# Attention on one core: three steps change engine, two places of waiting move, and two later stages load and square their rows in pieces

## The reference, cut to what matters

```python
x = x + attention_a(layernorm(x))      # changed: phase_attend
x = x + moe_ffn(layernorm(x))
x = x + attention_b(layernorm(x))      # changed: first loads (phase_route), squares and first loads (phase_final)
x = x + moe_ffn(layernorm(x))
```

```python
out_t = softmax(local_scores) @ v
pcs   = (softmax(causal_scores) * exp(index_decays)).sum(rows of a segment)
kv    = einsum(normalised_scan(pcs), k, v);  out_lin = q @ kv
y     = tw * out_t + (1 - tw) * out_lin
```

```python
o = o * rsqrt(mean(o * o, -1) + EPS) * norm_w      # 4 heads of 64 per token
o = o * silu(x @ w_g);  out = o @ w_o
```

## Time and profile before

| | |
|---|---|
| time of 3 runs, median (lowest to highest) | 2725.63 us (2721.02 to 2728.28) |
| the profiled execution: its own time, its span | 2726.8 us, 2725.1 us |
| busy over the span | PE 85%, DVE 72%, ACT 57%, POOL 45% |
| attention a | 137 us to 1289 us: 32 heads |
| phase_route | 1603 us to about 1722 us |
| phase_final | 2342 us to about 2436 us |

### The profile page before, as it was taken

One profiled execution on the slowest core, in us unless ns is written; L12 is line 12 of the kernel. 1 busy time (PEld: TensorE's weight loads), 2 busy tenths in 40 slices (PEclk: granted clock), 3 DMA queues, 4 the chain that ended last, 5 costly groups with the idle time before them and its releaser, 6 DMA issues. The chain is left out here.

```text
span 2725.1 us, 72677 instructions
## 1 busy us (share of the span) xinstructions
PE 2308.1 (85%) x27120; PEld 1534.0 (56%) x27120; DVE 1961.8 (72%) x4896; ACT 1543.3 (57%) x3579; POOL 1220.2 (45%) x2149
## 2 busy tenths in 40 slices
PE   8689999999999999997987944499999999678792
PEld 5444444444444444444765844377777777566681
DVE  6478888888888898886564656277777776477465
ACT  5467777777777777775352322266666665236230
POOL 3323333333333333334775536544444544247561
PEclk9879999999999999999998975599999999689896
DMA  6711111111112111110447645301111111443555
GB/s 218 241 39 38 38 38 37 32 35 34 38 38 65 38 38 38 32 37 9 152 157 200 228 156 178 119 21 47 47 49 49 50 39 32 166 159 132 155 157 198
DMA packets 187257, 243.43 MB, mean 89 GB/s; under 512 B 41256, under 2 KB 144565, under 8 KB 184992
## 3 DMA queue, kind: packets, MB, share of 16 engines
q1 hardware_dynamic: 160512, 182.07, 21.8%
q0 software_dynamic: 19872, 50.41, 5.4%
q10 hardware_dynamic: 6528, 6.31, 0.8%
HBM read 136.09 MB, written 106.50 MB: 89 GB/s over the span
## 5 line engine op out<-in xcount | busy, mean ns | idle before, releaser
L658 DVE TENSOR_REDUCE at_mn<-at_S 128x1 f32<-128x1024 f32 (+4 forms) x704 | 604.4, 878 | 118.3 <-PE at_S L767 118.0
L588 ACT ACTIVATE at_E<-at_S,at_mn 128x1024 f32<-128x1024 f32 (+4 forms) x704 | 591.4, 850 | 162.9 <-DVE at_mn L658 162.8
L807 PE MATMUL at_pcs<-at_E,at_c 128*32 128x256 f32 (+1 forms) x4864 | 432.9, 345 | 0.0
L767 PE MATMUL at_S<-at_sk,at_sq 96*128 96x512 bf16 (+3 forms) x1152 | 334.2, 354 | 48.6 <-ACT at_E L588 25.1
L540 POOL TENSOR_TENSOR at_kvo<-at_kh,at_vh 128x256 f32<-128x256 f32 x512 | 303.7, 627 | 0.1
L578 ACT ACTIVATE at_Tt<-at_S,at_mn 128x192 f32<-128x192 f32 x512 | 173.7, 422 | 134.1 <-DVE at_mn L648 134.1
L807 PEld LDWEIGHTS at_pcs<-at_E,at_c 128*32 128x32 f32 x4864 | 185.8, 108 | 86.5 <-issue 80.6
L520 POOL TENSOR_TENSOR at_fi<-at_f,at_inv 128x12 f32<-128x12 f32 x128 | 26.3, 206 | 443.0 <-DVE at_inv L675 443.0
L1287 POOL DMA_INDIRECT expert_out<-m_ysb,m_dst x158 | 155.4, 984 | 129.1 <-DVE m_dst L1465 115.8
L767 PEld LDWEIGHTS at_S<-at_sk,at_sq 96*128 96x128 bf16 x1152 | 78.5, 97 | 231.5 <-issue 92.3
L807 PE MATMUL at_pcs<-at_Tt,at_c 128*32 128x128 f32 x1024 | 208.7, 286 | 0.0
(11 more groups left out here) (392 smaller groups left out, 5552.6 us busy)
## 6 DMA issues: line engine op xcount, KB each, us to landing
m_xg<-expert_rows SPq DMA_DIRECT2D x158, 129.0 KB
at_sq<-q_parts SPq DMA_DIRECT2D x192, 64.0 KB, 2.3
at_sk<-k_parts SPq DMA_DIRECT2D x192, 64.0 KB, 2.2
memory_rows<-m_blank SPq DMA_DIRECT2D x8, 1032.0 KB, 4.5
gl_hx<-memory_rows SPq DMA_DIRECT2D x32, 258.0 KB, 3.5
m_wgu<-in_f_wgu SPq DMA_DIRECT2D x2, 4096.0 KB, 14.4
rt_yin<-expert_out SPq DMA_DIRECT2D x8, 1024.0 KB, 10.4
fn_yin<-expert_out SPq DMA_DIRECT2D x8, 1024.0 KB, 8.1
```

What stands on the lines that cost most here:

```text
L588: nc.scalar.activation(E[:, at:at + w], S[v % NS_B][:, 0:w], ACT.Exp, bias=mn[:, q, s, 1 + j:2 + j], scale=-1.0, accum_out=rs[:, q, s, 1 + ...
L658: nc.vector.tensor_reduce(mn[:, q, s, 1 + j:2 + j], S[v % NS_B][:, 0:w], AX.X, ALU.min).then_inc(s_mn, 1)
L767: ins = nc.tensor.matmul(S[v % NS_B][:, c:c + cw], sq[:, u, t * P:(t + 1) * P], sk[:, u, c0 + c:c0 + c + cw], start=True, stop=True)
L807: ins = nc.tensor.matmul(pcs[j * R:(j + 1) * R, cols[0]:cols[1]].rearrange("p (b c) -> p b c", c=P), lhsT, rhs, start=(n, j) not in touche ...
```

## The change

In `phase_attend`:

- The difference (minima minus top) goes from VectorE (`tops`) to GpSimd (`differences(g + 1)`, at the end of turn g).
- The copy of the turned tiles goes from VectorE (behind minima 2) to ScalarE (behind exponential 2).
- `factors(g)` goes from the end of turn g-1 to a place behind exponential 1 of turn g.
- `outputs(g)` goes from behind minima 3 to behind minima 4.

In `phase_final` the square becomes 16 activations of 64 columns, each with its sum, and the sum on VectorE goes. In `phase_final` and `phase_route` the first step's loads are issued tile by tile, and the first mix waits tile by tile. TensorE's order is the same before and after.

```diff
+            def differences(g):
+                pool.wait_ge(s_top, g + 1)
+                pool.tensor_tensor(diff[:, g % 2, :, :], mn[:, g % NQ, :, :],
+                                   top[:, g % 2, :].unsqueeze(2).to_broadcast([P, NQ, KK]), ALU.subtract
+                                   ).then_inc(s_diff, 1)
...
+            def keep_transposed(g):
+                act.wait_ge(s_TT, 2 * g + 2)
+                if g >= 2:
+                    act.wait_ge(s_O, g - 1)
+                nc.scalar.copy(TTs[:, g % 2, :], M[:, :]).then_inc(s_TTs, 1)
...
                     for k in range(1, 1 + last):
                         exps(g + 1, k)
+                        if k == 1:
+                            factors(g)
+                        if k == 2:
+                            keep_transposed(g)
...
-                    factors(g + 1)
...
                 for k in range(1, 1 + len(units[(g + 1) % NQ])):
                     minima(g + 1, k)
-                    if k == 2:
-                        keep_transposed(g)
                     if k == 3:
                         inverses(g)
+                    if k == 4:
                         outputs(g)
```

```diff
+                if n == 0:
+                    for t in range(G):
+                        sp.dma_start(o[:, 0, t, :], o_dram[t * P:(t + 1) * P, :]).then_inc(first_in[t], 16)
+                        sp.dma_start(yin[:, 0, t, :], yb[t * P:(t + 1) * P, :]).then_inc(first_in[t], 16)
+                    return
...
-                nc.scalar.activation(sq[:, n % 2, :], o[:, n % NB, :, :].rearrange("p t d -> p (t d)"), ACT.Square
-                                     ).then_inc(s_sq, 1)
+                for r in range(G * GH):
+                    ins = nc.scalar.activation(sq[:, n % 2, r * GV:(r + 1) * GV], o[:, n % NB, r // GH, r % GH * GV:(r % GH + 1) * GV],
+                                               ACT.Square, accum_out=ss[:, n % 2, r:r + 1])
+                ins.then_inc(s_sq, 1)
...
-                nc.vector.tensor_reduce(ss[:, n % 2, :], heads(sq[:, n % 2, :]), AX.X, ALU.add).then_inc(s_ss, 1)
```

More of the change, by code:

```diff
@@ L544, in products @@
                     ins.then_inc(s_kvo, 1)
+            differences(0)
             for g in range(NG):
@@ L554, in _ @@
                     products(n - 1, 10, NT)
+                if g + 1 < NG:
+                    differences(g + 1)
             products(NHEAD - 1, 5, NT)
@@ L615, in _ @@
                 exps(0, k)
-            factors(0)
             for g in range(NG):
@@ L629, in _ @@
                             keep_kvr(n - 1)
-                    factors(g + 1)
+            factors(NG - 1)
+            keep_transposed(NG - 1)
             keep_pcs(NHEAD - 1)
@@ L1674, in phase_route @@
         y_in = [m.sem(f"y_in{u}") for u in range(NB)]
+        first_in = [m.sem(f"first_in{t}") for t in range(G)]
         s_stat, s_var, s_rstd, s_hn = (m.sem(k) for k in ("stat", "var", "rstd", "hn"))
@@ L1805, in stats_of @@
                 u, t0 = n % NB, first_tile(n)
-                dve.wait_ge(y_in[u], (n // NB + 1) * 16)
+                if n:
+                    dve.wait_ge(y_in[u], (n // NB + (u > 0)) * 16)
                 for j in range(TOPK):
@@ L1810, in stats_of @@
                     for t in range(G):
+                        if n == 0 and j == 0:
+                            dve.wait_ge(first_in[t], 16)
                         nc.vector.scalar_tensor_tensor(acc[:, t0 + t, :], yin[:, u, t, j * D:(j + 1) * D],
@@ L2667, in phase_final @@
         o_in, y_in = ([m.sem(f"{k}{u}") for u in range(NB)] for k in ("o_in", "y_in"))
+        first_in = [m.sem(f"first_in{t}") for t in range(G)]
         h_in = [m.sem(f"h_in{u}") for u in range(2)]
-        s_g, s_silu, s_mix, s_sq, s_gated, s_ss, s_inv, s_y = (
-            m.sem(k) for k in ("g", "silu", "mix", "sq", "gated", "ss", "inv", "y"))
+        s_g, s_silu, s_mix, s_sq, s_gated, s_inv, s_y = (
+            m.sem(k) for k in ("g", "silu", "mix", "sq", "gated", "inv", "y"))
         s_T, s_yT, s_zmm, s_z = (m.sem(k) for k in ("T", "yT", "zmm", "z"))
@@ L2753, in mix @@
                 u = n % NB
-                dve.wait_ge(o_in[u], (n // NB + 1) * 16)
-                dve.wait_ge(y_in[u], (n // NB + 1) * 16)
+                if n:
+                    dve.wait_ge(o_in[u], (n // NB + (u > 0)) * 16)
+                    dve.wait_ge(y_in[u], (n // NB + (u > 0)) * 16)
                 for j in range(TOPK):
@@ L2759, in mix @@
                     for t in range(G):
+                        if n == 0 and j == 0:
+                            dve.wait_ge(first_in[t], 32)
                         nc.vector.scalar_tensor_tensor(o[:, u, t, :], yin[:, u, t, j * D:(j + 1) * D],
@@ L2770, in gate_rows @@
                                         silu[:, n % 2, :], ALU.mult).then_inc(s_gated, 1)
-            def sums(n):
-                dve.wait_ge(s_sq, n + 1)
-                if n >= 2:
-                    dve.wait_ge(s_inv, 2 * n - 3)
-                nc.vector.tensor_reduce(ss[:, n % 2, :], heads(sq[:, n % 2, :]), AX.X, ALU.add).then_inc(s_ss, 1)
             def norm(n):
@@ L2795, in _ @@
             gate_rows(0)
-            sums(0)
             mix(1)
@@ L2800, in _ @@
                     gate_rows(n + 1)
-                    sums(n + 1)
                 norm(n)
```

15 lines of the change are left out of this document (3 added, 12 removed).

## The result

| | before | after |
|---|---|---|
| median (lowest to highest) | 2726.95 us of 4 runs (2721.02 to 2728.78) | 2888.97 us of 4 runs (2887.68 to 2892.04) |
| span of the profiled execution | 2725.1 us | 2886.0 us |
| mean granted clock of TensorE | 0.922 | 0.904 |

The ratio is 1.06, with a 95% interval of 1.0583 to 1.0617: the change makes the kernel 162 us slower. The forecast was 2847 us and at most 2880.

What follows compares the result with a forecast made beforehand. Attention a was taken to run at a ring of window exponentials, scores and minima, not at VectorE. 127 us more there, 5 off in `phase_final` and 1 off in `phase_route` gave 2847 us, range 2780 to 2880.

Steps and rivals of the forecast that it cites:

- The ring: Attention a's loop: window exponentials (ScalarE), scores 3 to 5 (TensorE), minima 5 and 6 (VectorE); 35.29 us per four turns.
- The rival in which VectorE is the bound: Attention a: copy and difference come off each turn, 102 us, with 6 of the rest 2618 us; 5 in 100.
- The copy to ScalarE: Attention a: behind exponential 2 the copy makes `values` start 0.90, 1.25, 0.91 and 1.37 us later in the four turns.
- starts later by the same amount: TensorE's list behind `values`: scores 4, sums, scores 5 and scores 6 all shift by the full delay, without idle time before.
- Difference off VectorE: End of each attention turn: moving minima minus top to GpSimd takes 0.20 us off, bounds 0.10 and 0.30.
- Those end before the top comes: GpSimd in attention: the 3 us of products ahead of `differences` are over before VectorE's top, so GpSimd has time.
- Outputs behind minima 4: Attention: costs nothing at q = 1, 2, 3; at q = 0 `decayed` comes later, the turn 1.58 us longer.
- Factors later: Attention, behind exponential 1: total at about 579.4, minimum 3 ends about 579.9, so nothing is paid.
- `phase_final`: VectorE's 1.21 us sum goes, ScalarE's squares (at most 5.4 us) stay hidden: 5 us off; nothing taken for loads.
- `phase_route`: First load by tiles lets three of eight mixes start before the last tile is in: 1 us off.
- Half of the delay absorbed: Attention a: only half the lateness of `values` gets through, 64 us more, less 6: about 2784 us; 12 in 100.
- The factor chain: Attention: GpSimd's small steps take twice as long, the inverse comes 0.5 us late a turn: 2911 us; 4 in 100.

## Why the prediction was right in its direction and short in its size

**What bounds the kernel: right.** The ring of window exponentials, scores and minima held. VectorE lost 100 us of busy time (1961.8 to 1861.6) and the kernel grew. The rival in which VectorE is the bound (2618 us) is out: the copy was not on the path, `values` now is. VectorE's wait for scores grew to 2.9 us in a turn (186.1 in 65), more than the forecast's 2. The Trainium skill (Perfetto Trace Analysis, Optimizing Scalar/DVE Operations) says that moving work to ScalarE may make sense when VectorE is saturated. VectorE at 72% busy was not what the ring waited for, and the ratio is 1.06.

**The copy to ScalarE: the mechanism and its lateness right, the step that failed is here.** The lateness was forecast at accumulator read plus 0.84 us; in the turn shown it is 608.82 to 609.58, 0.76, plus 0.11 for the factors that stand ahead of exponential 2 already. At full clock the copy's place cost 1.00, 1.26, 0.86 and 1.38 us where 0.90, 1.25, 0.91 and 1.37 were forecast, and with the clock held up by three matmuls the four turns add up to 39.27 us where 39.3 was forecast. What failed is the sentence that everything behind `values` "starts later by the same amount". That holds only if TensorE runs as fast after the wait as before it. The trace of before gave a way to ask: TensorE had had no wait above 0.8 us in its loop, and that one in one turn of four, and its clock was at 1.00 there. I put 1.1 us of idle time into each turn and kept the clock, a term set at nothing without a reason. It fell in 39 turns, for 50 us. The span grew by 161 us where the sum said 121: these 50, less 3 in the loop at full clock (124 against 127) and less 7 that the other stages gave back beyond the forecast.

**Difference off VectorE: right in sign, too small.** Forecast 0.80 us a head (0.20 a turn); measured 1.31 (0.21, 0.32, 0.13, 0.67), together with the factors' move. The 0.20 was read in one turn and taken for all. From the start of the top to the start of what follows the difference it was 0.30, 0.39, 0.29 and 0.75 us before, in the turns with q = 1, 2, 3, 0, since the difference itself took 0.17, 0.27, 0.17 and 0.62. "Those end before the top comes", said of GpSimd's products, is wrong too: in the q = 0 turn top and difference fall in their middle, and in the turn that I read they ended 0.3 us behind the top's start. Most of the surplus is in the q = 0 turn.

**Outputs behind minima 4: the turn right, its parts not.** I priced the q = 0 turn 0.41 above the copy's lateness. Undone one at a time, the terms of that turn are 0.67 gained by the difference (0.20 forecast), 0.80 lost by the outputs (0.41) and 1.38 lost by the copy (1.37): from 8.53 to 10.04 us, where 10.11 was forecast. That the two errors cancel has a reason. The forecast worked the end of the turn out as one path, from the outputs through `decayed` to `normalise`, and the changed kernel shows it (`at_den` waits for TensorE in each such turn, 13.5 us in 16). The difference isn't on that path, so what it gains is lost again to the outputs. The sum fits, but the outputs' price is twice what the sum gives them. (It depends on the order: with the copy on ScalarE, the outputs back behind minima 3 give 0.98.)

**Factors later: right.** VectorE waits for nothing but scores and `decayed` from 574 to 1244 us. What the move is worth by itself was not run.

**`phase_final`: right, and a little too small.** A step took 8.12 us, as forecast (8.1). ScalarE and TensorE in the changed kernel:

```profile
2546.82 1.02 ACT L2744 ACTIVATE fn_silu<-fn_p_g 128x1024 f32<-128x1024 f32 x1 [2.33 <-PE fn_p_g L2843]
2547.74 0.25 ACT L2751 ACTIVATE fn_sq<-fn_o 128x64 f32<-128x64 f32 x1
2547.98 0.24 ACT L2751 ACTIVATE fn_sq<-fn_o 128x64 f32<-128x64 f32 x1
...
2554.93 1.02 ACT L2744 ACTIVATE fn_silu<-fn_p_g 128x1024 f32<-128x1024 f32 x1 [2.33 <-PE fn_p_g L2843]
...
2585.11 3.72 PE L2865 MATMUL fn_p_z<-ready_won,fn_yT 128*128 128x256 f32 x16 [1.22 <-ACT fn_yT L2763]
```

The squares stand 0.24 us apart, 3.8 for 16, where I allowed up to 5.4, and ScalarE still idles 2.33 us in a step, so they are hidden. The stage took 10 us less against 5: 5.6 in the steps, 1.5 at the start (the load by tiles, for which I took nothing), and about 3 in matmuls of the same shapes that ran shorter, above all the last projection but one with 3.72 us against 5.40 before. The row of before, and the granted clock (the number behind the five busy times) over this projection, before and after:

```profile
2423.71 5.40 PE L2847 MATMUL fn_p_z<-ready_won,fn_yT 128*128 128x256 f32 x16 [0.73 <-ACT fn_yT L2740]
```

```profile
2423.71:2429.11 5.40, 5.40 (x18) 4.49 (x19) 1.92 (x2) 0.00 (x0) 1.17 (x1) 0.68 0.00 0
2585.11:2588.83 3.72, 3.71 (x17) 3.09 (x18) 1.41 (x2) 0.00 (x0) 2.28 (x1) 1.00 0.00 0
```

Before, a stretch at half clock fell on it, and in the change none did, nor in the run with the edits outside attention alone. So here too a part that the sum lacks is the clock, this time as a gain. What kept it up there was not tried.

**`phase_route`: right.** 0.8 us less, 1 forecast.

**The rivals.** Half of the delay absorbed (2784 us): no, all of it got through, turn by turn as shown above. The factor chain (2911 us): near the time, but its mechanism did not occur. The case that happened, the full lateness and the clock besides, was not on the list.

## What to carry to other kernels

Before an instruction is moved to an idler engine, ask when that engine's list lets it start, and who is first to wait for it: here the same 0.6 us copy gave a ratio of 0.985 behind the window's exponentials and 1.064 two exponentials later, with the rest of the kernel alike. When an edit makes a busy TensorE idle inside a loop that ran at full clock, price the idle time and add the matmuls behind it at half clock as a case of its own; a few zero matmuls in the wait tell the two apart in one run. When a sum is made of terms of both signs, undo them one at a time, since a turn can come out right whose terms are each off by two.

## What the runs showed of the hardware

- A wait of 1.1 us on average for TensorE, with the engine busy on either side of it, stood in every turn; a granted clock of 0.50 followed in 39 of some 120 turns; with three matmuls of zeros in the wait it stayed at 1.00. What decides which turn is hit these runs do not settle.
- With the loop made shorter elsewhere (0.98 us in one turn of four), the trace has 53 such stretches instead of 39, and a mean head as long as without it (41.00 us against 40.98).
- A `tensor_tensor` of twelve columns on VectorE took 0.62 and 0.27 us in two turns beside GpSimd's products, each time to the end of the product that was running, and 0.17 without them.
- An activation of 64 columns with its sum took 0.24 us from start to start, where the 128-column one with its read had taken 0.34.
